# One VectorE reduction for both weighed chunks of a pair, in a cross-attention and RWKV kernel on one core

## What is computed

```python
def step(s, inp):
    k_l, v_l, w_l, r_l = inp
    a = k_l[..., :, None] * v_l[..., None, :]
    out = jnp.einsum('bhs,bhst->bht', r_l, faaaa * a + s)
    s_new = a + w_l[..., None] * s
    return (s_new, out)
_, outs = jax.lax.scan(step, s0, seq)
```

## Time and profile before

| what | value |
|---|---|
| median of 3 runs | 872.62 us (872.28 to 875.66) |
| the profiled execution | 872.65 us, its span 870.6 us |
| PE busy | 812.5 us (93% of the span) |
| PEld busy | 542.1 us (62%) |
| VectorE busy | 601.7 us (69%), 1110 instructions |
| ACT busy | 354.2 us (41%) |
| POOL busy | 295.6 us (34%) |
| mean granted TensorE clock | 0.992 of full speed |

### The profile page before, as it was taken

One profiled execution on the slowest core, in us unless ns is written; L12 is line 12 of the kernel. 1 busy time (PEld: TensorE's weight loads), 2 busy tenths in 40 slices (PEclk: granted clock), 3 DMA queues, 4 the chain that ended last, 5 costly groups with the idle time before them and its releaser, 6 DMA issues. The chain is left out here.

```text
span 870.6 us, 18064 instructions
## 1 busy us (share of the span) xinstructions
PE 812.5 (93%) x7370; PEld 542.1 (62%) x7370; DVE 601.7 (69%) x1110; ACT 354.2 (41%) x715; POOL 295.6 (34%) x281
## 2 busy tenths in 40 slices
PE   7799999799999999899998899989999899999997
PEld 4477568447664676447764577636775377457764
DVE  2475867896579836896389944898369976894441
ACT  1322336524562327424364144633364157225512
POOL 3043741383118510383106720185103921540000
PEclk9899999999999999999999999999999999999999
DMA  9830103000110001100011001100001000100000
GB/s 300 328 97 1 49 2 123 1 2 1 26 49 2 1 26 50 49 1 1 26 50 49 2 2 48 51 25 1 2 1 48 27 2 2 49 1 3 26 24 24
DMA packets 17026, 34.20 MB, mean 39 GB/s; under 512 B 2224, under 2 KB 3888, under 8 KB 16944
## 3 DMA queue, kind: packets, MB, share of 16 engines
q1 hardware_dynamic: 14048, 31.20, 10.4%
q10 hardware_dynamic: 2896, 1.86, 0.7%
HBM read 24.66 MB, written 8.39 MB: 38 GB/s over the span
## 5 line engine op out<-in xcount | busy, mean ns | idle before, releaser
L2061 POOL TENSOR_TENSOR xmix<-xmix,xa 128x512 f32<-128x512 f32 x80 | 94.1, 1197 | 172.8 <-DVE xmix L1567 172.8
L2074 POOL TENSOR_TENSOR prod<-RA,K 128x512 f32<-128x512 f32 x112 | 126.7, 1157 | 23.6 <-DVE RA L1631 20.7
L1240 ACT ACTIVATE st<-av,half 32x512 f32<-32x512 f32 x64 | 74.7, 1166 | 43.3 <-DVE av L1714 41.9
L625 PE MATMUL CH<-prod,ones 32*32 32x512 f32 (+1 forms) x1152 | 75.8, 582 | 10.2 <-DVE av L1661 8.9
L1661 DVE TENSOR_TENSOR av<-CH,vT 128x512 f32<-128x512 f32 x112 | 71.7, 681 | 12.5 <-PE CH L625 12.3
L1567 DVE SCALAR_TENSOR_TENSOR xmix<-PA,chan,sx 128x256 f32<-128x256 f32 x128 | 52.9, 475 | 39.0 <-PE PA L509 37.5
L1672 DVE TENSOR_REDUCE yred<-av 128x64 f32<-128x512 f32 (+2 forms) x112 | 70.9, 674 | 0.0
L718 PE MATMUL PC<-sq_Wo,y 128*128 128x512 f32 x128 | 61.5, 612 | 6.6 <-DVE y L1757 6.6
L525 PE MATMUL PC<-sqb,sq_fWk 128*128 128x256 f32 x256 | 60.6, 386 | 6.4 <-DVE sqb L1793 6.4
L2086 POOL TENSOR_TENSOR K<-K,W 128x512 f32<-128x512 f32 x8 | 15.3, 1915 | 143.4 <-DVE prod L1597 143.4
L525 PE MATMUL PB<-xmix,sq_Wk 128*128 128x256 f32 x256 | 61.7, 386 | 0.0
(11 more groups left out here) (163 smaller groups left out, 1388.4 us busy)
## 6 DMA issues: line engine op xcount, KB each, us to landing
x<-x_rows SPq DMA_DIRECT2D x11, 512.0 KB, 3.4
x<-in_x SPq DMA_DIRECT2D x8, 512.0 KB, 3.7
x_rows<-x SPq DMA_DIRECT2D x8, 512.0 KB, 4.2
out_x<-x SPq DMA_DIRECT2D x8, 512.0 KB, 2.8
ctx_t<-in_ctx SPq DMA_DIRECT2D x5, 512.0 KB, 3.8
y<-in_ctx SPq DMA_DIRECT2D x3, 512.0 KB, 8.3
sq_Wk<-in_square SPq DMA_DIRECT2D x1, 1024.0 KB, 13.5
sq_Wv<-in_square SPq DMA_DIRECT2D x1, 1024.0 KB, 16.9
```

Of the source, the lines that this page charges most:

```text
L625: mm = pe.matmul(out, ones16[rows, rows], v, start=True, stop=True)
L1240: act.activation(st[p, :, :, 32 * q:32 * q + S], src, ACT.Copy, scale=half[p, 0:1]).then_inc(st_ready, 1)
L2061: pool.tensor_tensor(m, m, xa[:, ct:ct + 2, 1:L + 1], ALU.add).then_inc(mix_ready, 1)
L2074: pool.tensor_tensor(by_pair(prod[:, g % 4, :], h), r, k, ALU.mult).then_inc(prod_pool, 1)
```

## The change

Where a level is 2 or more, the two reductions of a visit become one instruction over both slots of `av`: 1024 columns in, two pieces of `yred` out, one for each half. `b_reduce` is called once for a visit instead of once for a chunk. It waits until both chunks are weighed (`av_ready` at the end of the visit) and adds 2 to `red_ready`, so that all other waits on it keep their numbers. So that the first chunk of a pair (3, 5, 7, ..., all odd) lies in slot 0 and the second in slot 1, the slot number changes from g % 2 to (g + 1) % 2. Level 0 has no reduction and level 1 never had one; there nothing changes. 112 reductions of 512 columns become 56 of 1024.

```diff
-                dst = yred[:] if h == 1 else av[:, g % 2, :]
+                dst = yred[:] if h == 1 else av[:, (g + 1) % 2, :]
...
-            def b_reduce(u, g):
-                h, c = CHUNKS[g]
+            def b_reduce(u, begin, end):
+                h, c = CHUNKS[begin]
                 if h == 0:
                     return
-                dve.wait_ge(av_ready, N_CHUNKS * u + g + 1)
+                dve.wait_ge(av_ready, N_CHUNKS * u + end)
                 if h > 1:
                     n = CHUNK // h
                     if c == 0:
                         dve.wait_ge(yint_ready, len(INTRA) * u + INTRA.index(h))
-                    dve.tensor_reduce(yred[:, c * n:(c + 1) * n], by_pair(av[:, g % 2, :], h), AX.X, ALU.add).then_inc(red_ready, 1)
-                if c == h - 1:
+                    o = yred[:].rearrange("p (two m) -> p two m", two=2)[:, :, c * n:(c + 1) * n]
+                    dve.tensor_reduce(o, av[:].rearrange("p two (n j) -> p two n j", j=h), AX.X, ALU.add).then_inc(red_ready, 2)
+                if h == 1 or c == h // 2 - 1:
                     if h > 1:
-                        dve.wait_ge(red_ready, N_RED * u + g + 1 - FIRST[2])
+                        dve.wait_ge(red_ready, N_RED * u + end - FIRST[2])
                     o = halves(yint[:], h, 1)
                     dve.tensor_tensor(o, o, yred[:].rearrange("p (n h) -> p n h", h=h), ALU.add).then_inc(yint_ready, 1)
...
                     for g in range(begin, end):
                         b_weigh(u, g)
-                    for g in range(begin, end):
-                        b_reduce(u, g)
+                    b_reduce(u, begin, end)
```

## The result

The changed kernel takes 875.21 us (median of 21 runs, 872.8 to 877.31), the kernel before 872.89 us (21 runs, 872.01 to 875.66). The ratio is 1.0023, with an interval of 1.0015 to 1.003: some 2.0 us slower, with all of the interval above 1. That lies within 0.5%, in the range and in the class that was forecast, but it is well over twice the +0.75 us of the sum.

A forecast was written before the change was run, and what follows sets the result against it. PE is busy 93% of the span, but in each iteration's 41 us of chunk work PE and VectorE take turns in being late. Fifteen pairs on the path at +0.05 us add +0.75 to 872.65: 873.4 us, range 871.7 to 875.5.

The forecast's parts named there:

- The pair: Two weighings and their reduction on VectorE: 0.11 us later start, 0.06 us saved by joining, so +0.05 us each.
- The length: A joint reduction of 1024 columns takes 1208 ns, by the line through 512 and 2048 columns, without stretching by POOL.
- Where PE takes it: In each of five iterations PE's waits of 0.36 and 0.92 us grow by 0.05, 0.94 stays: 0.50 us.
- The drain: Batches 6 and 7: +0.10 us in batch 6, +0.10 at batch 7's output projection, +0.05 at its 0.92 us wait.
- The tightest place, 771.20: Drain, chunks 11 and 12 weighed directly behind reductions: weighing could start at 771.15, just in time; otherwise 0.1 us once.
- The fill: In the fill PE does not wait for VectorE at all after the first reductions, so the cost is 0.
- VectorE's busy time: Over the whole span VectorE's busy time falls by 7.8 us, to near 594 us.
- 1: Rival: the added wait is free, only instruction count matters; -0.06 us for a pair, 871.7 us; chance 0.12.
- 2: Rival: two output pieces make the joint reduction as long as two, 1.35 us; up to 875.5 us; chance 0.12.
- 3: Rival: longer PE waits bring the clock down once in each iteration, 8.5 us more, 881.9 us; chance 0.04.
- 4: Rival: the path gains more than counted, pairs up to 0.14 us shorter, -2.1 us, 870.5 us; chance 0.04.
- 5: Rival: the changed kernel doesn't do what it says; no size given, next to no weight.

The follow-up runs named there:

- the probe: Kernel before plus five short VectorE sequences at its end, varying output pieces and signal: reductions start 0.10 us after the weighing's end with signal 2, 0.04 with 1.

## Why the prediction was right, and where its sum was off

- **The direction and its cause**: right. The overlap lost by the wait is worth more than the instruction removed; the wait alone makes the whole of it.
- **The pair**: mis-sized, and with it every term of the sum. The sum had 1.30 us to the reduction's start and 1.13 from there on. The second is exact. The first is 1.40. Of the 0.10 between them, 0.02 is in the kernel before too (two weighings take 1.29 there); 0.08 is left, as the row that I took the 0.03 us from (the addition into `yint`) signals 1 and the new reduction 2. So +0.14, not +0.05, where both wait and work behind it are on the path.
- **The length**: 1219 ns against 1208, fine. POOL does not stretch it.
- **Where PE takes it**: one of the two places in an iteration. The wait of 0.92 grew by 0.13. That of 0.36 did not: the step failed by counting only instructions, when the addition into `yint`, one row behind the reduction, is tied to POOL's rows and gave back what it lost. 0.94 stayed, as said. Five times 0.13 is 0.65 us, near the predicted 0.50 by luck: two errors that cancel.
- **The drain**: the largest failure. It was priced at 0.25 us and costs 1.3 (0.24 in batch 6, 0.12 up to the next wait for `av`, 0.97 in batch 7). The tightest place, 771.20, was said to be just in time and is 0.11 late: the weighing starts 0.11 behind the reduction's end (773.63 + 1.22 to 774.96 above), and the row of before showed 0.13 at that very place (769.80 + 1.27 to 771.20), where I had put 0.03. And I had not looked at what else has a partner in time: L1778 was 0.10 us ahead of POOL's update. Said was that POOL would not stretch the reductions, true, but not what it does to the instruction behind them. What the half clock in batch 6 does was not priced; it comes without the change too, so it is not a term that was missing. The clock was a rival in the iterations, where it stayed at 1.00.
- **The fill**: nothing, as said, though not for the reason given. PE does wait for VectorE behind the first reductions, 2.52 us for L1578 at 159.02, and waits the same 2.52 after the change (162.16).
- **VectorE's busy time**: 602.7 instead of 594 us. The profile's busy time counts an overlap once, not twice (it gives the 112 reductions of before 70.9 us, where 112 x 0.675 is 75.6), so the 7.8 us were never there to be saved.
- **The rivals**: 1 (a free wait, and with it the rule that only the number of operations counts) is refuted by the kernel with the wait alone, which has as many operations as before and loses 0.2%. 2 is refuted by 1219 ns. 3 is not seen: the clock is at 1.00 in all five iterations. 4 is refuted, as none of the three waits is shorter, and 5 by the 56 joint reductions in their places. The measured 875.2 lies at the top of the range, 875.5, for other reasons than the one that set it: the range was set by a dear reduction, and it is L1778 in batch 7 and the pair's larger price that came near it. That it held is in part luck.

## What to carry to other kernels

Before two instructions become one, look at what the first of them overlapped with: an operation that may start before its neighbour has ended gives that up when it must wait for it, and here that cost 0.13 us (0.20 with a signal of 2), where the removed instruction gave some 0.06. Then walk the instructions behind it and ask of each what it is tied to: one that ends with another engine swallows a delay of a tenth of a microsecond, and one that starts a tenth ahead of an instruction of another engine that it contends with turns it into 0.7. And give the signal of a short instruction an increment of 1: by the probe that is worth 0.06 us each time, though no whole kernel with it was run. Last, before a stretch at half clock is charged to a change, look for it in other profiles of the kernel without the change.

## What the hardware showed that I had not expected

- A signal that rises by 2 starts its own VectorE instruction 0.06 us later (0.10 us behind the end of the weighing that it waits for, against 0.03 to 0.04 with 1).
- VectorE's step L1778, one input and 512 columns, takes 0.54 us if it starts 0.10 to 0.12 us ahead of POOL's addition into the key, which then takes 1.38 to 1.39; 1.24 to 1.39 us if it starts between 0.01 us ahead and 0.13 us behind, and POOL's then takes 1.09. POOL loses 0.30 us in the one case, VectorE 0.7 in the other. The Trainium skill, SBUF — State Buffer, section "SBUF: two separate sides", says this of the port pair that the two engines share: for a VectorE instruction in a 2-port mode or with two SBUF inputs, whoever starts first has it for the whole instruction. No run here shows which mode L1778 is in, but the rows are what that would give: its end, 778.74, lies 0.29 us behind POOL's end at 778.45. The case with a lead of 0.01 us, which still loses, shows that the recorded start is not exactly the moment that decides.
- All 56 joint reductions lie within 1219 to 1221 ns, whatever POOL does beside them.
- The half clock behind one and the same idle time of 3.35 us, with the same order of instructions around it, lasted 0, 3.4 and 6.8 us in different profiles, and batch 6 took 29.23, 29.31 and 30.46 us.
